# A fused AdaLN attention and feed-forward block on one core: another order at the start, and the third head's projections as seven block products

## The reference

```
ada = cond @ ada_w + ada_b                      # 8 x 1536: shift1, scale1, gate1, shift2, scale2, gate2
x1  = ln(x) * (1 + scale1) + shift1
qkv = x1 @ qkv_w + qkv_b                        # 16 heads of 128
att = softmax(q @ k.T * 128**-0.5) @ v
x   = x + gate1 * (att @ out_w + out_b)
x2  = ln(x) * (1 + scale2) + shift2
x   = x + gate2 * (gelu(x2 @ w1 + b1) @ w2 + b2)   # 1024 hidden
h   = relu(x @ ternary(W_fc).T) ** 2               # ternary: groups of 64, sign times mean size
y   = x_in + rms_norm(h) @ ternary(W_proj).T
```

## Time and profile before

| | |
|---|---|
| median of 3 runs | 350.53 us |
| the profiled execution's own time | 350.69 us |
| its span, first to last instruction | 348.9 us |
| PE busy | 342.3 us (98%) |
| DVE, ACT, POOL busy | 222.4, 220.2, 148.7 us |
| all DMA | 16.53 MB, 47 GB/s over the span |

### The profile page before, as it was taken

One profiled execution on the slowest core, in us unless ns is written; L12 is line 12 of the kernel. 1 busy time (PEld: TensorE's weight loads), 2 busy tenths in 40 slices (PEclk: granted clock), 3 DMA queues, 4 the chain that ended last, 5 costly groups with the idle time before them and its releaser, 6 DMA issues.

```text
span 348.9 us, 5879 instructions
## 1 busy us (share of the span) xinstructions
PE 342.3 (98%) x1950; PEld 293.7 (84%) x1950; DVE 222.4 (64%) x386; ACT 220.2 (63%) x560; POOL 148.7 (43%) x140
## 2 busy tenths in 40 slices
PE   8999999999999999999999999999999999999995
PEld 7888888889888888888888888888787788889884
DVE  6676756553555664456466454585875788577796
ACT  2773565667576657756664675667579536876593
POOL 3571329736534964644595573479341100000000
PEclk9999999999999999999999999999999999999998
DMA  6953003100300320030020002020000000000002
GB/s 176 362 192 120 3 0 120 62 1 3 120 0 0 120 60 0 0 120 0 25 95 0 0 6 115 0 62 0 4 0 2 0 2 0 0 2 1 1 32 90
DMA packets 12338, 16.53 MB, mean 47 GB/s; under 512 B 720, under 2 KB 8992, under 8 KB 12320
## 3 DMA queue, kind: packets, MB, share of 16 engines
q1 hardware_dynamic: 12136, 16.16, 14.2%
q10 hardware_dynamic: 184, 0.15, 0.1%
HBM read 15.25 MB, written 1.05 MB: 47 GB/s over the span
## 4 chain that ended last, share of the span: by engine, by line
PE 74%; issue 20%; DVE 3%; ACT 1%; POOL 1%; POOLq 0%; ACTq 0%
PE bank L1228 16%; PE bank L1230 16%; PE bank L1229 16%; PE bank L1315 8%; PE bank L1298 8%; PE bank L1304 4%; PE bank L1427 2%; PE bank L1442 1%; DVE yT L976 1%; DVE yT L966 1%; PE bank L1463 1%; PE bank L1422 1%; DVE yT L962 0%; ACT prob L579 0%; ACT hbuf L718 0%
## 5 line engine op out<-in xcount | busy, mean ns | idle before, releaser
L391 POOL TENSOR_TENSOR prob<-prob,rinv 128x512 f32<-128x512 f32 x32 | 36.2, 1131 | 60.3 <-DVE rinv L1025 59.9
L579 ACT ACTIVATE prob<-bank,negmax 128x128 f32<-128x128 f32 x128 | 45.4, 365 | 25.6 <-DVE negmax L1012 25.6
L1315 PEld LDWEIGHTS bank<-probT,vals 128*128 128x128 f32 x256 | 33.3, 191 | 3.2 <-issue 0.8
L952 DVE SCALAR_TENSOR_TENSOR o_lo<-bank,bias,o_hi 128x512 fp32r<-128x512 f32 x32 | 23.9, 745 | 17.2 <-ACT o_hi L532 17.2
L532 ACT ACTIVATE o_hi<-bank,bias 128x512 fp32r<-128x512 f32 x32 | 21.9, 686 | 19.4 <-PE bank L1315 19.4
L1315 PE MATMUL bank<-probT,vals 128*128 128x128 f32 x256 | 33.9, 275 | 0.0
L350 POOL TENSOR_TENSOR wqk_lo<-raw_qk,wqk_hi 128x512 fp32r<-128x512 f32 x16 | 21.2, 1323 | 19.6 <-ACT wqk_hi L493 18.1
L488 POOL TENSOR_TENSOR xr<-raw_qk,xt 128x256 f32<-128x256 f32 x1 | 0.7, 721 | 67.2 <-ACT raw_qk L796 67.2
L1012 DVE TENSOR_REDUCE negmax<-bank 128x4 f32<-128x512 f32 x32 | 21.8, 682 | 7.9 <-PE bank L1298 7.9
L1228 PE MATMUL bank<-wv_hi,x_hi 128*128 128x512 f32 x62 | 26.1, 420 | 0.0
L579 ACT ACTIVATION_READ_ACCUMULATOR prob<-bank,negmax 128x1 f32 x128 | 26.0, 203 | 0.0
(11 more groups left out here) (218 smaller groups left out, 974.1 us busy)
## 6 DMA issues: line engine op xcount, KB each, us to landing
raw_qk<-in_L_cond_qkv_w_dram SPq DMA_DIRECT2D x6, 512.0 KB, 4.6
raw_v<-in_L_cond_qkv_w_dram SPq DMA_DIRECT2D x4, 512.0 KB, 4.1
raw_o<-in_L_cond_out_w_dram SPq DMA_DIRECT2D x4, 512.0 KB, 3.5
t_w<-in_L_cond_ada_w_dram SPq DMA_DIRECT2D x1, 1024.0 KB, 8.9
raw_w<-in_L_cond_ffn_w_dram SPq DMA_DIRECT2D x2, 512.0 KB, 6.9
t_raw<-in_L_ffn_W_fc_dram SPq DMA_DIRECT2D x4, 256.0 KB, 3.7
t_raw<-in_L_ffn_W_proj_dram SPq DMA_DIRECT2D x4, 256.0 KB, 3.8
raw_qk<-in_L_cond_ffn_w_dram SPq DMA_DIRECT2D x1, 1024.0 KB, 4.9
```

Source lines behind the costliest of these rows:

```text
L391: nc.gpsimd.tensor_tensor(e, e, rinv[:, j % 2, :].unsqueeze(2).broadcast_to([P, SQ, P]), ALU.mult).then_inc(norm_done, 1)
L579: e = nc.scalar.activation(prob[:, j % 2, s, :], bank[BS][:, s * P:(s + 1) * P], ACT.Exp, bias=negmax[:, j % 2, s:s + 1], accum_out=rowsum ...
L952: nc.vector.scalar_tensor_tensor(out=lo[:, :], in0=bank[BO][:, :], scalar=bias[:, bass.ds(HG * G + VB + j % HG, 1)], in1=hi[:, :].bitcast( ...
L1315: m = nc.tensor.matmul(bank[BO][:, s * P:(s + 1) * P], vals[:, b, h], probT[:, s, :], start=True, stop=True)
```

## The change

The start: ACT now issues the 512 KB of modulation weights first, then the condition and the four bias rows that SP issued; SP keeps both halves of x, takes the modulation bias row, and waits for the first half of x only before it issues the first head's weights. On PE there are 3 and 1 products of the identity where there were 7, and the last three are gone; both bias transposes stand ahead of the modulation products. The normalised x is transposed feature half by feature half, half 1 first; ACT and DVE each modulate two sequences of each half (`modulate_first`), and `first_qk` interleaves Q and K of the first head. A `wv_lo` part moves from POOL to DVE, and half of the copy of raw x from ACT to DVE.

The third head: group 0's head 2 uses the seven block products. `weight_sums` takes two heads at once, and `x_sums` moves ahead of DVE's unit (0, 1).

The end: the sum with x is a step of its own (`add_x`) with a signal per feature half; for quad 1 the gate moves one chunk later and the sum another, and the transposes move from chunk 5 to chunk 6.

```diff
@@ sync
-            sp.dma_start(ada_w1, ada_w[:, 0:2 * D].rearrange("(k p) n -> p k n", p=P)).then_inc(ada1_in, 16)
-            sp.wait_ge(x0_in[1], 16)
+            sp.dma_start(arow, ada_b.rearrange("(n p) -> n p", p=P)).then_inc(arow_in, 16)
+            sp.wait_ge(x0_in[0], 16)
...
-            for src, at, n in ((qkv_b, QB, 3 * H), (out_b, OB, KD), (ffn_b1, F1B, NC), (ffn_b2, F2B, KD)):
-                sp.dma_start(brow[at - NA:at - NA + n, :], src.rearrange("(n p) -> n p", p=P)).then_inc(bias_in, 16)
@@ gpsimd
-            for k in range(KD):
-                wv_lo_part(k, k + 1)
+            wv_lo_part(0, 1)
...
-            weight_sums(0, 3, 4, 0)
+            weight_sums(0, 2, 4, 0)
@@ scalar
+            def modulate_first():
+
+                act.wait_ge(ada_ready, 1)
+                for k, src, full, hi in ((1, bank[7], m1_a, hi1_a), (0, bank[6], mod_a, xs_hi)):
+                    act.wait_ge(xt0_done, KD - k)
+                    for b in range(SQ // 2, SQ):
+                        m = nc.scalar.activation(xq0[:, k, b * P:(b + 1) * P], src[:, b * P:(b + 1) * P], ACT.Identity,
+                                                 bias=ada[:, SHIFT1 + k, b:b + 1], scale=ada[:, SCALE1 + k, b:b + 1])
+                    m.then_inc(full, 1)
+                    act.wait_ge(full, 1)
+                    hi_part(x_hi[:, k, SQ // 2 * P:SQ * P], xq0[:, k, SQ // 2 * P:SQ * P], hi)
...
+            act.dma_start(ada_w1, ada_w[:, 0:2 * D].rearrange("(k p) n -> p k n", p=P)).then_inc(ada1_in, 16)
             act.dma_start(crow, cond).then_inc(cond_in, 16)
-            act.dma_start(arow, ada_b.rearrange("(n p) -> n p", p=P)).then_inc(arow_in, 16)
+            for src, at, n in ((qkv_b, QB, 3 * H), (out_b, OB, KD), (ffn_b1, F1B, NC), (ffn_b2, F2B, KD)):
+                act.dma_start(brow[at - NA:at - NA + n, :], src.rearrange("(n p) -> n p", p=P)).then_inc(bias_in, 16)
...
+            ws_hi_part(0, 2)
+            o_hi_part(0, 0)
+            copy_p1(0, 2)
             ws_hi_part(0, 3)
-            o_hi_part(0, 0)
-            keep_k0(2, 5)
+            copy_u2(0, 2)
+            copy_u3(0, 2)
+            pair_k0(0, 2)
@@ vector
+            def add_x(quad):
                 dve.wait_ge(xT_done, quad + 1)
+                dve.wait_ge(xT1_done, 1)
                 for c in range(KD):
                     dve.wait_ge(gate_mul, KD * quad + c + 1)
-                    m = nc.vector.tensor_tensor(yT[:, c, cols(quad)], yT[:, c, cols(quad)], xT[:, c, cols(quad)], ALU.add)
-                m.then_inc(gated, 1)
+                    nc.vector.tensor_tensor(yT[:, c, cols(quad)], yT[:, c, cols(quad)], xT[:, c, cols(quad)], ALU.add).then_inc(gated, 1)
...
-            modulate(0, SHIFT1, SCALE1, bank[0:2])
-            dve.wait_ge(small_cp, 4)
+            modulate_first()
+            dve.wait_ge(wv_h, 2)
+            nc.vector.tensor_tensor(wv_lo[:, 1, :], raw_v[:, 1, :], wv_hi[:, 1, :].bitcast(F32), ALU.subtract).then_inc(wv_l, 1)
+            dve.wait_ge(xraw_mm, 1)
+            nc.vector.tensor_copy(xT[:, 1, cols(0)], bank[BS][:, :]).then_inc(xT1_done, 1)
+            dve.wait_ge(small_cp, 3)
             keep_q0(0, 0, 1)
...
             modulate(1, SHIFT1, SCALE1, bank[6:8])
+            x_sums()
             unit(0, 1)
...
+                if c == 2:
                     gate_y(1)
-                if c == 5:
+                if c == 3:
+                    add_x(1)
+                if c == 6:
                     dve.wait_ge(gt_mm, 2)
                     stats_of(3)
@@ tensor
+            keep_awake(3)
             pe.wait_ge(arow_in, 16)
-            nc.tensor.transpose(bank[6][:, 0:NA], arow, ident[0:NA, 0:NA]).then_inc(small_t, 1)
+            nc.tensor.transpose(bank[6][:, 0:NA], arow, ident[0:NA, 0:NA])
+            pe.wait_ge(bias_in, 64)
+            nc.tensor.transpose(bank[6][:, NA:NBIAS], brow, ident[0:NBIAS - NA, 0:NBIAS - NA]).then_inc(small_t, 1)
...
-            keep_awake(7)
-            pe.wait_ge(small_cp, 2)
+            keep_awake(1)
+            pe.wait_ge(small_cp, 1)
             pe.wait_ge(ada1_in, 16)
             ada_product(0, GATE1, ada_w1, bank[5])
...
-            qk_products(2, 0, 0)
+            pair_p1(0, 2)
+            pair_p2(0, 2)
+            ada_product(GATE1 + 4, GATE1 + 6, ada_w2, bank[7])
+            pair_p6(0, 2)
+            pair_p5(0, 2)
+            pair_p7(0, 2)
             ada_product(GATE1 + 6, GATE1 + 8, ada_w2, bank[7])
...
+            pair_p4(0, 2)
+            pair_p3(0, 2)
...
-                if c == 5:
+                if c == 6:
                     pe.wait_ge(xT_done, 2)
                     transpose_y(1)
-                if c == 6:
                     pe.wait_ge(t_done, NG)
```

More of the change, by code:

```diff
@@ L871, in modulate, with modulate_first @@
                 dve.wait_ge(mod_d, e + 1)
-                if e:
-                    split_lo(quad, KD * e)
-                else:
-                    nc.vector.tensor_copy(x_hi[:, 1, cols(quad)], xf[:, 1, :]).then_inc(x01_hi, 1)
-                    dve.wait_ge(x01_hi, 1)
-                    x_lo_part(quad, 1, xf)
-                    dve.wait_ge(xs_hi, 1)
-                    x_lo_part(quad, 0, xf)
+                split_lo(quad, KD * e)
+            def modulate_first():
+                dve.wait_ge(ada_ready, 1)
+                for k, src, full, hi in ((1, bank[BO], m1_d, hi1_d), (0, bank[BV], mod_d, hi0_d)):
+                    dve.wait_ge(xt0_done, KD - k)
+                    for b in range(SQ // 2):
+                        m = nc.vector.tensor_scalar(xq0[:, k, b * P:(b + 1) * P], src[:, b * P:(b + 1) * P],
+                                                    ada[:, SCALE1 + k, b:b + 1], ada[:, SHIFT1 + k, b:b + 1], ALU.mult, ALU.add)
+                    m.then_inc(full, 1)
+                    dve.wait_ge(full, 1)
+                    nc.vector.tensor_copy(x_hi[:, k, 0:SQ // 2 * P], xq0[:, k, 0:SQ // 2 * P]).then_inc(hi, 1)
+                dve.wait_ge(hi1_d, 1)
+                dve.wait_ge(hi1_a, 1)
+                x_lo_part(0, 1, xq0)
+                dve.wait_ge(hi0_d, 1)
+                dve.wait_ge(xs_hi, 1)
+                x_lo_part(0, 0, xq0)
             def x_lo_part(quad, k, xf=xfull):
@@ L1038, in unit @@
                     gate_y(0)
+                    add_x(0)
                 if j == 1 and not second:
@@ L1472, in _, with first_qk @@
             transpose_raw(0, (bank[BE], bank[BS]))
-            keep_awake(3)
-            def first_query():
+            def first_qk():
+                dsts = (bank[BQ], bank[BK])
                 pe.wait_ge(wqk_h, 1)
-                for k, ready in ((1, x01_hi), (0, xs_hi)):
-                    pe.wait_ge(ready, 1)
-                    nc.tensor.matmul(bank[BQ][:, :], wqk_hi[:, k, 0:P], x_hi[:, k, cols(0)], start=k == 1, stop=False)
-                pe.wait_ge(wqk_l, 1)
                 for k in (1, 0):
-                    nc.tensor.matmul(bank[BQ][:, :], wqk_lo[:, k, 0:P], x_hi[:, k, cols(0)], start=False, stop=False)
-                for n, k in enumerate((1, 0)):
-                    pe.wait_ge(xs_lo, n + 1)
-                    m = nc.tensor.matmul(bank[BQ][:, :], wqk_hi[:, k, 0:P], x_lo[:, k, cols(0)], start=False, stop=k == 0)
-                m.then_inc(q_mm, 1)
+                    if k:
+                        pe.wait_ge(hi1_d, 1)
+                        pe.wait_ge(hi1_a, 1)
+                    else:
+                        pe.wait_ge(hi0_d, 1)
+                        pe.wait_ge(xs_hi, 1)
+                    for w in (wqk_hi, wqk_lo):
+                        if w is wqk_lo:
+                            pe.wait_ge(wqk_l, 1)
+                        for n in range(2):
+                            nc.tensor.matmul(dsts[n][:, :], w[:, n * KD + k, 0:P], x_hi[:, k, cols(0)],
+                                             start=k == 1 and w is wqk_hi, stop=False)
+                for k in (1, 0):
+                    pe.wait_ge(xs_lo, KD - k)
+                    for n, done in ((0, q_mm), (1, k_mm)):
+                        m = nc.tensor.matmul(dsts[n][:, :], wqk_hi[:, n * KD + k, 0:P], x_lo[:, k, cols(0)], start=False, stop=k == 0)
+                        if k == 0:
+                            m.then_inc(done, 1)
             def first_values():
@@ L1537, in transpose_y @@
             def transpose_y(quad):
-                pe.wait_ge(gated, quad + 1)
-                for s in range(SQ):
-                    for c in range(KD):
+                for c in range(KD):
+                    pe.wait_ge(gated, KD * quad + c + 1)
+                    for s in range(SQ):
                         m = nc.tensor.transpose(bank[BACK[quad][s // 2]][:, (s % 2) * D + c * P:(s % 2) * D + (c + 1) * P],
```

103 lines of the change are left out of this document (43 added, 60 removed).

## The result

The changed kernel takes 355.21 us (median of 4 runs, 354.76 to 355.57) against 350.2 us before (4 runs, 349.86 to 351.02): a ratio of 1.0141, 95% interval 1.0122 to 1.0161. It is slower by 5 us, and that lies above the range of the prediction. The profiled execution took 355.56 us, its span 353.8 us.

The account below looks back on a forecast made before the run. PE, busy 342.3 of 348.9 us, was taken to bound the kernel. Terms +1.4 + 0.15 - 0.1 - 0.4 = +1.05 us gave 351.5 us beside the median 350.53; the 8-in-10 range was 349.0 to 353.2.

Parts of the forecast that it names:

- The first term, T: Start: T, when transposes of the normalised x begin, moves from 9.60 to 11.0 us: +1.4 us (ends -0.5 and +2.7).
- my latest end: Start: the condition's latest landing, behind everything, at 6.3 us; earliest 3.96, taken 5.3.
- two counts of work: Start: clock rises at 12.0 us if 6.7 us of work must be redone, 9.1 if 3.8; middle taken, 10.6.
- The rival in which the clock stays low: Start: condition at 6.3 us, product slow throughout, half the first eight transposes too; sum +2.8, 353.2 us; chance 0.18.
- The second term, from T on: From x's transposes to the second quad's: DVE's longer chain makes PE wait, spending the interleaving's saving; +0.15 us (-0.3 to +0.5).
- The third head: Group 0's head 2: three fewer matmuls save 0.68 us, waits at joins cost 0.55; -0.1 us (-0.68 to +0.6).
- my unfavourable end: Third head: +0.6 us, if what `p6` needs comes another ACT pass of 0.69 us late.
- The end: Last part: gain at `yT` given back at the next normalised x, gelu wait goes; -0.4 us (0 to -0.5).
- the ends that I gave them: Limits per term: start -0.5 and +2.7; after it -0.3 and +0.5; third head -0.68 and +0.6; end 0 to -0.5.

Follow-up runs that it names:

- queues only: The kernel before with only the new DMA order (weights first on ACT, then condition and biases; x and modulation bias on SP): 356.49 us against 349.89.
- five fillers: The kernel before with the end's change and five instead of seven fillers ahead of the modulation product: median 349.18 us against 350.29, ratio 0.9988.
- the first part by itself: The changed kernel with weights third on SP and the third head back to 24 matmuls, rearranged start and end kept: 352.01 us against 350.01.
- the first four experiments: Kernel before with new DMA order 356.49 us, without seven fillers 352.49; changed kernel with condition issued first 353.5, with eleven fillers 352.49; each against 349.89.

## Why the prediction was wrong, step by step

**The first term, T: the step that failed, by its size.** I put it at +1.4 us, with the condition at 5.3 us and the clock at 10.6. Measured: +3.06, the condition at 6.37 and the clock at 17.76. The mechanism was right (a small transfer held behind a large one, and a gap that costs the clock): the queue's order alone brought the wait into the kernel before, and taking out fillers alone cost that kernel its early rise. Two choices within it were wrong:
- I took the landing between its ends by rate, at 309 GB/s. The two queues together moved 86 and 171 GB/s in the stretches of 2 to 4 us where one had moved 255 and 298, and the condition did not land in proportion but with the weights ahead of it: my latest end. (With the condition first the two moved 236 and 364.)
- I took the clock's rise as the middle of two counts of work. It did not come with the modulation product (3.3 us at the slow pace) nor with the transposes of x behind it, but only after 11 us of busy PE, from 6.42 to 17.76 us. The rival in which the clock stays low named the right mechanism and the right T within 0.4 us (12.3), and sized the rest too small: half of the first eight transposes, where all sixteen and the first four of twelve projection matmuls ran slow.

The Trainium skill, "DMA: Bandwidth & Descriptors", section "Issuing engines are not separate DMA queues", says that a second issuing engine adds no engine to carry the data. The runs agree: the weights landed at 6.1 us from the head of their own queue and at 6.3 from third place behind x.

**The second term, from T on: +0.15 forecast, +1.65 measured** (0.93 to the first scores, 0.72 to the second quad). I had nothing in it for a clock that stays low past T, and the 0.93 goes with that. With the old order of work this stretch grew by 0.87 us with the clock rising 2.7 us behind T (queues only), and by 1.86 with the clock rising 4.7 us behind it (five fillers). The changed kernel, with its clock 5.1 us behind T, lost 0.93, so the new order, without three fillers there, seems to give back some 0.9; no run has the new order at the higher clock throughout. The 0.72 I had placed in the wrong engine. My sum for it was wrong too: 5.13 - 1.23 + 1.3 + 0.1 puts `qT` at T + 5.3, not T + 5.6, and leaves nothing beyond the cover of 0.44.

I followed DVE, whose two passes took 1.67 and 0.68 us where I had put 0.65 each; but PE was not late for DVE. It waited for `wqk_lo` on POOL, which waited for `wqk_hi`, which in ACT's program now stands behind the first head's K. That move stood in the order of ACT's instructions and I did not follow it. Taking the slow pass off DVE gained nothing, and the wait (0.33 to 0.45 us) was there in every version with the rearranged start, except the one with the condition first, where PE waited 0.3 us for the normalised second quad instead. That ACT's order is the cause is read from the chain of waits; no run puts `wqk_hi` back ahead of K.

The Trainium skill, "GPSIMD Engine Reference", section "8. Key points", says that GpSimd contends with DVE instructions that have two inputs in SBUF. The traces agree: such a pass took 1.67 us beside a POOL pass of 1.29 us, and takes 0.68 us with POOL idle.

**The third head: -0.1 forecast, +1.03 measured, +0.59 alone.** The saving of 0.68 us was right and the joins were in the right places. They cost 1.3 us beyond what the plain order has, where I had summed 0.55: each also holds a piece that no wait lists, and I had no stall at `p5`, where PE waits for `k1T` behind DVE's passes, one of them 1.76 us long beside a POOL pass. Alone the term reached my unfavourable end, +0.6; in the changed kernel it went beyond, by 0.4 us that no experiment takes apart.

**The end: -0.4 forecast, -0.89 measured, -0.97 alone.** The gain at `yT` was given back, as forecast, though behind `o_lo` (at 254.1 us in the run with the end alone) and not at the next normalised x. The gelu's idle time gave 0.75 us and not 0.4.

**The sum.** 3.06 + 1.65 + 1.03 - 0.89 = 4.85 us of span, and 355.56 - 350.69 = 4.87. All four terms lay beyond the ends that I gave them, three on the slow side and the end's on the fast one. The range stopped at the middle of the slow rival (its own sum gives 353.3, not 353.2), which let the held condition and the slow clock add up but kept the other three terms near nothing.

## What to carry to other kernels

A transfer of a few KB that gates the first work goes ahead of everything large in its queue: behind 512 KB the condition came 2.5 us later here. Look also at what starts beside a large transfer: issued at the same moment as x, the weights came 0.2 us sooner and x 2 to 3 us later, and issued 0.7 us after it they did no harm. Dummy matmuls ahead of the first work earn their place by the clock and not by what they compute: leaving seven out cost 2.6 us by the medians, with all four runs slow, and leaving two out, with no wait opened, cost 3 us in four runs of twelve. With filler over PE's early waits all twelve runs of the rearranged start lay within 0.8 us. When a step moves in one engine's program, look at what now stands behind it on that engine and who feeds on that, before counting what the step itself saves; and of a sum with fewer products, count each join at an engine's pass plus the start of the next matmul.

## What the runs showed of the hardware

- The granted clock fell during the modulation product or just behind it, at 9.37, 8.57 and 8.95 us, in three kernels in which PE had no wait over 0.73 us since 1.52 us. Rises in the twelve experiments and the changed kernel lie between 5.16 and 17.76 us.
- The same program can catch or miss the early rise from run to run (8 of 12 runs are in the lower group with five fillers, 3 of 10 with the first part by itself), worth 2 to 3 us; twelve runs with filler in place of the waits stayed within 0.8 us. One of eight runs of the kernel before, beside the first four experiments, took 354.15 us where the others took 349.50 to 350.39. That the lower groups are runs with an early rise is inferred: no trace of one was taken for those kernels, and what decides it in a run stays open.
- Two queues that start together with 512 KB each moved 27, 86 and 171 GB/s in the stretches from 1 to 4 us (35, 176 and 219 in the kernel with the queues only), against 33, 255 and 298 with one loaded queue. With the second queue's 512 KB issued 0.66 us later, behind 8 KB, the two moved 19, 236 and 364.
- A DVE pass over two SBUF tiles of 128x512 took 0.68 us with POOL idle and 1.67 to 1.76 us beside a POOL pass.
